# Experts on tokens sorted by expert, in place of every expert on every token

## The reference

```python
h = _layernorm(x, axis=-1) * (1 + ca) + sa
x = x + ga * _L0_attn_ref(h, ...)
h = _layernorm(x, axis=-1) * (1 + cb) + sb
x = x + gb * _L0_ffn_ref(h, ...)
...
probs = jax.nn.sigmoid(x @ router_w.T + expert_bias[None, :])
top_w, top_idx = jax.lax.top_k(probs, 8)
top_w = top_w / (jnp.sum(top_w, axis=-1, keepdims=True) + 1e-09) * 2.5
combine = zeros.at[jnp.arange(T)[:, None], top_idx].set(top_w)
h1 = jax.nn.silu(jnp.einsum('th,eih->eti', x, w_gate))
routed = jnp.einsum('eti,ehi->th', h1 * combine.T[:, :, None], w_down)
shared = jax.nn.silu(x @ w_gate_shared.T) @ w_down_shared.T
```

## Time and profile before

| | |
|---|---|
| runs | 979.15, 979.62, 998.62 us; median 979.62 us |
| profiled execution, span from the first to the last instruction | 977.4 us |
| PE busy | 940.8 us (96% of the span) |
| DVE busy | 770.3 us (79%) |
| ACT busy | 681.3 us (70%) |
| POOL busy | 402.8 us (41%), nothing after the router |
| DMA | 160.57 MB, mean 164 GB/s |

### The profile page before, as it was taken

The page is one execution under the profiler, slowest core; times in us unless marked ns, Lnnn a source line. Parts: engine busy times, 40 slices in busy tenths (PEclk is TensorE's granted clock), DMA queues, the critical chain, the costliest instruction groups (busy, mean ns, idle before and its releaser), DMA issues.

```text
span 977.4 us, 15761 instructions
## 1 busy us (share of the span) xinstructions
PE 940.8 (96%) x4592; PEld 684.4 (70%) x4592; DVE 770.3 (79%) x1450; ACT 681.3 (70%) x1171; POOL 402.8 (41%) x265
## 2 busy tenths in 40 slices
PE   4899999999999999999997999999999999999997
PEld 2656666666666666666543888888888888888886
DVE  5866766766676676676764999999999999999996
ACT  4656666666666666666655777877777777777775
POOL 0688888898888888898900000000000000000000
PEclk9999999999999999999999999999999999999999
DMA  7957644544553563454105999999999999999992
GB/s 217 235 161 202 166 115 103 130 100 117 130 122 78 125 152 92 104 130 101 47 18 139 224 221 220 220 219 220 218 218 220 217 219 217 221 216 220 219 218 61
DMA packets 71633, 160.57 MB, mean 164 GB/s; under 512 B 10416, under 2 KB 36336, under 8 KB 61856
## 3 DMA queue, kind: packets, MB, share of 16 engines
q1 hardware_dynamic: 70816, 158.66, 72.8%
q10 hardware_dynamic: 768, 1.31, 0.4%
HBM read 105.60 MB, written 2.42 MB: 111 GB/s over the span
## 4 chain that ended last, share of the span: by engine, by line
PE 88%; DVE 5%; ACT 3%; issue 2%; DMA 1%; POOL 1%; ACTq 0%; SPq 0%; DVEq 0%
PE ps L635 44%; PE ps L439 11%; PE ps L426 11%; PE ps L415 5%; PE ps L417 5%; PE ps L389 5%; PE ps L452 2%; PE ps L400 2%; ACT prob L729 1%; DVE prob L1032 1%; POOL prob L904 1%; DMA strips<-comb_rows 0%; DVE PT L208 0%; PE ps L374 0%; PE ps L485 0%
## 5 line engine op out<-in xcount | busy, mean ns | idle before, releaser
L904 POOL TENSOR_SCALAR prob<-prob,rinv 128x512 f32<-128x512 f32 x256 | 398.1, 1568 | 87.8 <-DVE rinv L1049 85.7
L729 ACT ACTIVATE prob<-prob,nmax 128x512 f32<-128x512 f32 x256 | 183.0, 716 | 138.7 <-DVE nmax L1032 138.6
L635 PE MATMUL ps<-hT,wT 128*128 128x512 f32 x960 | 243.9, 390 | 1.3 <-ACT oT L820 1.3
L1235 DVE TENSOR_TENSOR PT<-v_sb,strips 128x1024 f32<-128x1024 f32 x160 | 196.1, 1225 | 44.0 <-ACT v_sb L871 33.6
L871 ACT ACTIVATE v_sb<-ps 128x1024 f32<-128x1024 f32 x160 | 164.6, 1029 | 90.2 <-PE ps L635 89.9
L635 PEld LDWEIGHTS ps<-hT,wT 128*128 128x128 f32 x960 | 180.4, 188 | 40.5 <-issue 3.0
L635 PE MATMUL ps<-stack,wT 128*128 128x512 f32 x640 | 197.8, 391 | 4.3 <-DVE wT L1222 4.3
L208 DVE COPY PT<-ps 128x512 f32<-128x512 f32 x128 | 88.4, 691 | 135.4 <-PE ps L426 133.0
L1222 DVE TENSOR_TENSOR wT<-PT,stack 128x1024 fp32r<-128x1024 f32 x160 | 195.0, 1219 | 0.0
L863 ACT CAST stack<-PT 128x1024 fp32r<-128x1024 f32 x160 | 166.6, 1041 | 2.9 <-DVE PT L1235 2.9
L426 PEld LDWEIGHTS ps<-ident,prob 128*128 128x128 f32 x1024 | 114.4, 141 | 74.5 <-POOL prob L904 51.0
(11 more groups left out here) (113 smaller groups left out, 726.8 us busy)
## 6 DMA issues: line engine op xcount, KB each, us to landing
strips<-comb_rows SPq DMA_DIRECT2D x152, 512.0 KB, 12.8
stack<-qk SPq DMA_DIRECT2D x128, 256.0 KB, 3.8
k_low<-qk SPq DMA_DIRECT2D x64, 128.0 KB, 3.8
hT<-qk SPq DMA_DIRECT2D x64, 128.0 KB, 3.7
strips<-bias_rows SPq DMA_DIRECT2D x8, 896.0 KB, 5.6
strips<-in_L_ffn_w_gate SPq DMA_DIRECT2D x80, 64.0 KB, 11.2
strips<-in_L_ffn_w_down SPq DMA_DIRECT2D x80, 64.0 KB, 12.9
strips<-comb_rows SPq DMA_DIRECT2D x16, 256.0 KB, 5.7
```

The lines of the kernel that those rows point to most:

```text
L635: last = nc.tensor.matmul(ps[:, bank + c, :], weights(a), rows(m, c), start=start and k == 0, stop=stop and k == 2, skip_group_check=True)
L729: nc.scalar.activation(prob[:, u, :], prob[:, u, :], ACT.Exp, bias=nmax[:, u:u + 1], scale=-1.0, accum_out=rsum[:, u:u + 1]).then_inc(s_ex ...
L904: nc.gpsimd.tensor_scalar(prob[:, u, :], prob[:, u, :], rinv[:, u:u + 1], None, ALU.mult).then_inc(s_prob, 1)
L1235: nc.vector.tensor_tensor(weighted[:, k % 4, :], silu[:, k % 2, :], cb[:, r, half * HALF:(half + 1) * HALF], ALU.mult).then_inc(s_mul, 1)
```

## The change

The dense loop over experts goes. After routing, each token's row is written eight times, once for each of its experts, into `sorted_rows` in DRAM, which is cut into blocks of 128 rows. Expert e owns block e; rows beyond its first 128 go to further blocks ("spilled"), whose number is fixed for the worst case. With all four batches in one group there are 16,384 rows, 160 own blocks and 128 spilled ones, 288 blocks or 36.9 thousand rows of 512 B. Blocks that get no row are multiplied all the same, on zeros.

- During attention SP fills `sorted_rows` with zeros (18 DMAs of up to 16 blocks, two at the head of each `stack_pair` round). POOL sets the zeros and some constants first of all.
- `keep_top` now leaves a mask and the scaled weights. `count` (PE) counts the tokens of each expert, `spill_blocks` (DVE) and `sum_spills` (PE) turn counts into block numbers, `find_owners` and `copy_owners` list the expert that owns each spilled block, `rank` (PE) numbers the tokens of an expert, and `destinations` (DVE) makes the row number for each token and choice. `pick_weights` (DVE) collects the eight weights of a token.
- POOL modulates the normalised rows (`modulate_rows`) and scatters them: one indirect DMA for each of 16 tiles of 128 tokens and each of 8 choices.
- 36 steps of 8 blocks follow, 20 with own blocks and 16 with spilled ones. SP loads the blocks (512 KB) and the weights. Own weights are two DMAs of 256 KB; for spilled blocks SP reads the owner from SBUF into a register for each block (`value_load`) and loads 128 rows of 768 B from `expert_rows`, an array in which gate and down weights stand side by side. PE transposes the 8 blocks (f32), multiplies by the gate weights (64 columns wide, 128 tokens), ACT takes the silu, PE multiplies by the down weights, ACT and DVE copy, SP stores the results over the blocks. Products are single f32 matmuls, with no split into parts.
- POOL gathers the eight results of each token (16 x 8 indirect DMAs), DVE multiplies by the weights, sums, and adds to x. The shared expert is added to x before.

The core of the diff:

```diff
+class Group:
+    def __init__(self, batches, pad):
...
+        self.extra = -(-worst_extra(S * len(batches)) // STEP) * STEP
+        self.blocks = E + self.extra
...
+GROUPS = (Group((0, 1, 2, 3), 0),)
+STEPS = [(g, n, n >= E) for g, group in enumerate(GROUPS) for n in range(0, group.blocks, STEP)]
+NX, NW, NY, NGATHER = 6, 5, 3, 8
...
@@ SP
+            sp.wait_ge(s_zero, 1)
             for b in range(B - 1):
                 for n in range(2, HPAIRS + 2):
+                    fill(2 * (b * HPAIRS + n - 2))
+                    fill(2 * (b * HPAIRS + n - 2) + 1)
...
+            def load_weights(s):
...
+                if s >= NW:
+                    sp.wait_ge(s_down, s - NW + 1)
+                if not spilled:
+                    sp.dma_start(weights[:, r, 0:STEP * I], gate_t_in[:, ...]).then_inc(s_wl[r], 16)
+                    sp.dma_start(weights[:, r, STEP * I:STEP * I + STEP * I], down_pairs[:, ...]).then_inc(s_wl[r], 16)
+                    return
+                for j in range(STEP):
+                    at = owner_at[g] + first - E + j
+                    expert = sp.value_load(owner[0:1, at:at + 1], min_val=0, max_val=E - 1)
+                    sp.dma_start(weights[:, r, j * 192:(j + 1) * 192],
+                                 expert_rows[bass.ds(expert * P, P), :]).then_inc(s_wl[r], 16)
...
+            def load_blocks(s):
...
+                if first == 0:
+                    sp.wait_ge(s_scatter[g], 16 * len(GROUPS[g].tiles) * TOPK)
+                if s >= NX:
+                    sp.wait_ge(s_xt, 2 * (s - NX + 1))
+                sp.dma_start(x_blocks[:, s % NX, :, :], block_rows[g][:, first:first + STEP, :]).then_inc(s_x[s % NX], 16)
...
+            for s in range(len(STEPS)):
+                store_blocks(s)
+                if s + NW < len(STEPS):
+                    load_weights(s + NW)
+                if s + NX < len(STEPS):
+                    load_blocks(s + NX)
@@ PE
-            round_of(0, True)
-            with pe.Fori(1, rounds) as i:
-                round_of(i, False)
...
+            count(0)
+            sum_spills(0)
+            rank(0)
+            find_owners(0)
...
+            transpose_blocks(0)
+            for s in range(len(STEPS)):
+                gate(s)
+                if s + 1 < len(STEPS):
+                    transpose_blocks(s + 1)
+                if s >= 1:
+                    down(s - 1)
+            down(len(STEPS) - 1)
@@ POOL
+            def scatter(b):
...
+                for n in range(QT * b, QT * (b + 1)):
+                    for k in range(TOPK):
+                        nc.gpsimd.indirect_dma_start(
+                            sorted_rows[g], bass.IndirectOffsetOnAxis(ap=dest[:, n, k:k + 1], axis=0), rows[:, n, :],
+                            None).then_inc(s_scatter[g], 16)
+            def pick(g):
+                for r in range(NY):
+                    pool.wait_ge(s_y[r], 16 * len(range(r, LAST_STEP[g] + 1, NY)))
+                for n in GROUPS[g].tiles:
+                    if n >= NGATHER:
+                        pool.wait_ge(s_fin, n - NGATHER + 1)
+                    for k in range(TOPK):
+                        nc.gpsimd.indirect_dma_start(
+                            picked[n % NGATHER][:, k, :], None, sorted_rows[g],
+                            bass.IndirectOffsetOnAxis(ap=dest[:, n, k:k + 1], axis=0)).then_inc(s_pick[n % NGATHER], 16)
@@ DVE
+            def combine(n):
...
+                then(nc.vector.tensor_tensor(product, got, wts[:, n, :]..., ALU.mult))
+                then(nc.vector.tensor_reduce(acc[:, n % 2, :], product.rearrange("p k d -> p d k"), AX.X, ALU.add))
+                then(nc.vector.tensor_tensor(acc[:, n % 2, :], acc[:, n % 2, :], mod_rows[:, 2, b, :], ALU.mult))
+                nc.vector.tensor_tensor(x_tile, x_tile, acc[:, n % 2, :], ALU.add).then_inc(s_fin, 1)
```

More of the change, by code:

```diff
@@ L194, in adaln_block @@
+        s_ya, s_yd = sem("results_copied_act"), sem("results_copied_dve")
+        s_y = [sem(f"results_stored{r}") for r in range(NY)]
+        s_pick = [sem(f"results_picked{r}") for r in range(NGATHER)]
+        s_fin, s_out = sem("final"), sem("stored")
         QKV_STEPS = (0, 2, 4, 1, 3, 5)
@@ new lines, in count @@
+            def count(g):
+                group = GROUPS[g]
+                pe.wait_ge(s_mrowc, 2 + g)
+                pe.wait_ge(s_kept, group.batches[-1] + 1)
+                for half, experts in enumerate((slice(0, P), slice(E - P, E))):
+                    for n in group.tiles:
+                        last = nc.tensor.matmul(ps[:, 0, half * P:(half + 1) * P], masks[:, n, experts], ones[:, :],
+                                                start=n == group.tiles[0], stop=n == group.tiles[-1],
+                                                skip_group_check=True)
+                last.then_inc(s_cnt, 1)
@@ new lines, in gate @@
+            def gate(s):
+                r, spilled = s % NW, STEPS[s][2]
+                pe.wait_ge(s_wl[r], weight_target(s))
+                pe.wait_ge(s_xa, s + 1)
+                pe.wait_ge(s_xd, s + 1)
+                if s >= 2:
+                    pe.wait_ge(s_silu, s - 1)
+                for j in range(STEP):
+                    at = j * 192 if spilled else j * I
+                    last = nc.tensor.matmul(ps[(j % 2) * I:(j % 2 + 1) * I, GATE[s % 2], (j // 2) * P:(j // 2 + 1) * P],
+                                            weights[:, r, at:at + I], xT[:, s % 2, j * P:(j + 1) * P],
+                                            start=True, stop=True, skip_group_check=True)
+                last.then_inc(s_gate, 1)
@@ L881, in _ @@
[L881 to L895 removed]
+            copy_mod_rows(2)
@@ L1089, in norm2 @@
                 dve.wait_ge(s_rstd2, b + 1)
+                if b == 0:
+                    dve.wait_ge(s_fill, 16 * sum(-(-group.width // NT) for group in GROUPS))
                 norm(b, xn2)
@@ L1254, in _ @@
[L1254 to L1260 removed]
+            keep_top(3)
+            spill_blocks(0)
+            destinations(0)
+            copy_owners(0)
+            for b in range(1, B):
+                destinations(b)
```

649 lines of the change are left out of this document (371 added, 278 removed).

## The result

The changed kernel takes 1156.1 us (median of 3 runs, 1154.18 to 1159.11) against 979.62 us: a ratio of 1.1777, 95% interval [1.1696, 1.1857]. Slower was the forecast's likeliest case, and the time lies in its range, 46 us above the predicted 1110. The profiled execution took 1159.11 us, with a span of 1157.1 us.

A forecast was written before the change was run, and what follows sets the result against it. PE bound the expert stage (432 us), with DMA nearly full beside it. Replacing it by a serial chain: 540 + 3 + 128 + 6.6 + 107 + 183 + 4.4 + 128 + 2.2 + 3.1 + 2.7 = 1108, plus 2.2: 1110 us; range 920 to 1340.

The forecast's parts named there:

- hand-over: Between scatter and steps: last scatter lands 2.2 us after issue, a 512 KB load takes 4.4 us; 6.6 us.
- 36 steps: Expert steps: 20 with ordinary weights at 5.8 us, less 10, make 107 us; 16 with spilled weights make 183 us.
- end: After the last gather: landing 2.2 us, combination of the last tile 3.1, output landing 2.7.
- The indirect DMAs: Scatter and gather on POOL: 256 indirect DMAs at 1.0 us each, 128 us for each pass.
- Rival 1: Scatter and gather: POOL issues at SP's 0.34 us, two passes cost 87 instead of 256 us, time 941; chance 0.25.
- rival 2: Scatter and gather: POOL pays a round trip of 2.2 us for each DMA, time 1417; chance 0.1.
- The 16 slow steps: Steps with spilled weights: SP's eight reads and issues, block load and store take 11.4 us a step, 183 in all.
- the 0.75: Spilled steps: us taken for SP's read of an expert's number into a register, between 0.029 and 2.1 us.
- Attention: First stage, 0 to 500 us: 18 fills of zeros add between 0 and 23 us; 3 taken.
- PE late in the attention stage: Sign that the prediction is wrong; it expected dense DMA in the first nine head pairs without PE falling behind.
- Routing: Between attention and scatter: top 8, counting, ranking and destinations, from 500 to about 540 us.
- PE at 1.2 GHz after its rest: Expert steps: sign that the prediction is wrong, steps bound by PE at that clock after its long rest.

The follow-up runs named there:

- the first two experiments: Against the changed kernel, each indirect DMA moved 64 of 128 rows (1143.1 us), or rows of 256 B in place of 512 B (1161.67 us).
- the third and fifth experiments: Against the changed kernel: spilled steps loading fixed weights without reading owners, 1043.03 us; reads and loads of spilled weights split between ScalarE and SP, 1080.71 us.
- The fourth experiment: Against the changed kernel, the two fills of a pair issued after the copy into `hcur`, not before it: 1150.52 us.
- The combined version: Changed kernel with two groups, reads split between SP and ScalarE, owners read ahead, fills behind the copy: 987.26 us, ratio 1.0029.

## Why the prediction was right, and where it was off

The chain in series was foreseen, with its two waits, and the order of its parts is the trace's. Its steps against the profiled span:

| step | forecast | measured | from |
|---|---|---|---|
| up to the first scatter | 543 | 554.3 | timeline of POOL |
| scatter | 128 | 171.3 | 554.26 to 725.57 |
| hand-over | 6.6 | 6.0 | first transpose of a block at 731.58 |
| 36 steps | 107 + 183 | 251.7 | last store issued at 983.25 |
| last store | 4.4 | 3.8 | first gather at 987.07 |
| gather | 128 | 160.9 | last gather issued at 1147.98 |
| end | 8.0 | 9.1 | 1157.1 |
| sum | 1108 | 1157.1 | |

*The indirect DMAs* hold the error: 171.3 + 160.9 against 256, 76 us too little. The value that I took from POOL's smallest arithmetic step came out right for the instruction (0.94 to 0.99 us), but by luck: the row was of another operation, and my reason, work over 128 indices, fell in the first two experiments. And my sum set them edge to edge, where the trace has 0.30 us between two and 2.11 us now and then. Rival 1 (0.34 us) and rival 2 (2.2 us, in sequence) both fell: a transfer still lands 2.2 to 2.5 us after its issue, but the next is issued after 1.27 to 1.35. The Trainium skill's 2.0 us plus bytes ("DMA: Bandwidth & Descriptors", Anatomy of one DMA — SWDGE (gpsimd) path) thus agrees with the landing of one and is no pitch for a row of them; 256 B rows in place of 512 B changed nothing here.

*The steps* are 38 us shorter than forecast. The first 16 stores are out by 798.73, 67 us after the first transpose: the full DMA gave 399 GB/s in these steps, not 270, and a step took 3.8 us and not 5.8. The other four ordinary steps do not show at all, since SP loads five steps ahead: the chain has 16 ordinary periods, 16 of eight reads by SP and a tail of 7.1 us, not 20 and 16. I had taken a middle between the two speeds of the earlier trace rows, and the faster one was itself too low for large plain rows. The 16 slow steps were right in mechanism and size: 177.4 us, 11.1 each, against 183 and 11.4, and the third and fifth experiments show that SP's reads set them. Eight reads with their issues took 10.2 us on average against 10.24, and the block load and the store 0.96 against 1.2. The close agreement in the reads is in part luck: the 0.75 stood on no row, seven of eight reads with their issues take 1.11 us and not 1.28, and one in each step takes 2.2. For a register load the Trainium skill ("DMA: Bandwidth & Descriptors", Latency and other measured facts) has a floor of about 600 ns. The trace differs: such a load takes 0.27 us by the median, and the next instruction of SP starts 0.30 us after it.

*Attention* was forecast to lose 3 us to the fills and lost 11.7. I costed the fills against free DMA time and the slack of the stack copies, and did not name the copy into `hcur`, which has no such slack: it stands right behind two of the fills on SP's queue and PE waits for it. The fourth experiment gave 8.1 us of it back. "PE late in the attention stage" was one of the prediction's signs of being wrong, and in this it was. *Routing* took 41.5 us from there to the first scatter, against 39.

*Net of all:* 76 + 11 us too little, 38 too much. That the number lies only 46 us off is thus in part luck: two errors of opposite sign. The mechanism, a chain in series with a price for each indirect DMA and each read, was right. PE at 1.2 GHz after its rest, the doubt that closed the prediction, did not set the steps: in those with spilled weights PE, at a granted clock of 0.56, was busy for half of the time only, and with the owners gone they ran 3.8 us apart. For the kernel before, 432 us were at stake, and scatter, steps and gather, laid end to end, took 584 (171.3 + 251.7 + 160.9). The combined version shows that the plan itself can be level: hiding half of both passes, halving SP's chain, reading the owners ahead and ordering the fills took 169 us off. A second group hides half a scatter and half a gather (86 + 81 us) and adds 20 steps at 3.8 us, since the weights and the padded blocks are moved once more; alone it won 78 us. What it wins beside the other parts, no run shows. What is left then is DMA bandwidth in the steps and the two passes' exposed halves.

Left open: what the 0.30 and 2.11 us between indirect DMAs are (the long pauses go mostly with the number of rows and grow beside the steps' transfers; the cause was not tested), what the long second read of a step waits for, and whether fewer, longer instructions exist for the two passes.

## What to carry to other kernels

An operation that replaces dense arithmetic by data movement is to be priced per instruction and in sequence: count the indirect DMAs and the register-addressed loads, multiply by their pitch (not their duration), and ask what stands beside them; here PE was busy for 38 of the 352 us of the two windows in which POOL issued the indirect DMAs. Where a chain runs group by group, a group boundary is what lets one group's moves hide under another's products, as long as the weights read again cost less than what they hide. And a bulk transfer off the path is placed behind, never ahead of, the small copy that someone waits for on the same queue.

## What the runs showed of the hardware that was not expected

- An indirect DMA on POOL costs nearly the same for 64 or 128 rows (0.930 and 0.987 us in the scatter) and for 256 or 512 B a row (0.989 and 0.987); 0.30 us follow each. In the changed kernel's scatter, pauses of 2.11 us begin at 590.82, 630.20, 667.36 and 704.52, 28 instructions from one to the next. With 64 rows there are two pauses, 51 instructions apart; with 256 B a row there are four as before; beside the steps of the two-group run they last 5.64 and 6.42 us.
- A read of a register from SBUF on SP with the issue of the DMA behind it takes 1.11 us by the median, and once in nearly every step 2.2.
- 512 KB transfers in and out with 256 KB of weights in large pieces ran at 399 GB/s in the changed kernel and at up to 413 in the run without the owners; the highest slice before had been 376.
